# R loaded through POOL's queue, its spread moved up on DVE, and thirteen identity products on PE before the first projection

## The reference, cut to what matters

```
q, k, v = (split_heads(xn @ W.T + b) for W, b in ((Wq, bq), (Wk, bk), (Wv, bv)))     # xn = layernorm(x)
feature_map(t) = exp(t/sqrt(8) @ R - 0.5 * sum((t/sqrt(8))**2))                       # R is 8 x 8
q1, k1 = feature_map(q), feature_map(k)
kv = einsum('bhnd,bhne->bhde', k1, v);  z = 1 / (sum(q1) + 1e-8)
x = x + merge(einsum('bhnd,bhde,bhn->bhne', q1, kv, z)) @ Wo.T + bo
x = x + cross(layernorm(x), experts(slots(layernorm(x))))
```

## Time and profile before

| what | us |
|---|---|
| median of the three runs | 193.84 |
| the profiled execution | 194.13 |
| its span, first to last instruction | 192.3 |
| PE busy | 176.7 (92%) |
| POOL busy | 140.7 (73%) |
| DVE busy | 135.7 (71%) |
| ACT busy | 117.4 (61%) |

### The profile page before, as it was taken

How to read it: one execution, slowest core, us unless ns; L and a number is a source line. 1 busy time by engine, 2 the same in 40 slices (tenths; PEclk the granted TensorE clock), 3 DMA queues, 4 the chain that set the end, 5 groups by cost and what they waited for, 6 DMA issues and landing times.

```text
span 192.3 us, 4773 instructions
## 1 busy us (share of the span) xinstructions
PE 176.7 (92%) x1495; PEld 131.1 (68%) x1495; DVE 135.7 (71%) x399; ACT 117.4 (61%) x292; POOL 140.7 (73%) x278
## 2 busy tenths in 40 slices
PE   0798879999999999999999976999998999999993
PEld 0435567778876777777878755732665699888992
DVE  2668958797877887869786634637527999979850
ACT  2235357796779858776977562236413876765871
POOL 4488969879789986899276695305957869687983
PEclk9999999999999999999999997599999999999999
DMA  4839968999990000000000000000000000201113
GB/s 108 239 101 366 362 152 262 346 349 335 367 311 14 0 3 2 3 0 3 0 3 0 2 5 0 0 3 0 3 0 0 0 27 32 84 29 59 55 56 111
DMA packets 19675, 18.25 MB, mean 95 GB/s; under 512 B 1289, under 2 KB 15458, under 8 KB 19650
## 3 DMA queue, kind: packets, MB, share of 16 engines
q1 hardware_dynamic: 18802, 17.35, 28.7%
q10 hardware_dynamic: 848, 0.59, 1.4%
HBM read 15.84 MB, written 2.10 MB: 93 GB/s over the span
## 4 chain that ended last, share of the span: by engine, by line
PE 75%; POOL 11%; DVE 3%; issue 3%; DMA 3%; ACT 2%; ACTq 1%; POOLq 0%; DVEq 0%
PE ps L1131 11%; PE ps L1203 8%; PE ps L1372 6%; PE ps L1418 5%; PE ps L1241 4%; PE ps L1310 4%; PE ps L1184 4%; PE ps L1141 4%; PE ps L1164 3%; PE ps L1154 3%; PE ps L1406 3%; DMA X<-in_L_attn_x_dram 3%; PE ps L1395 2%; PE ps L1195 2%; PE ps L1174 2%
## 5 line engine op out<-in xcount | busy, mean ns | idle before, releaser
L1131 PE MATMUL ps<-Wproj,xnT 128*128 128x512 f32 x64 | 32.5, 633 | 1.0 <-ACT Wproj L544 0.5
L508 POOL TENSOR_TENSOR Wgs<-Wgs,W2s 128x256 f32<-128x256 f32 x31 | 18.7, 628 | 1.5 <-DVE W2s L1030 1.5
L1131 PEld LDWEIGHTS ps<-Wproj,xnT 128*128 128x128 f32 x64 | 11.4, 198 | 10.0 <-issue 8.6
L1418 PE MATMUL ps<-W1s,W2s 128*128 128x128 f32 x128 | 17.3, 279 | 0.7 <-ACT W2s L705 0.7
L1418 PEld LDWEIGHTS ps<-W1s,W2s 128*128 128x128 f32 x128 | 15.8, 191 | 2.2 <-ACT W2s L705 1.8
L1203 PE MATMUL ps<-XN2T,Ad 128*128 128x256 f32 x64 | 16.7, 384 | 0.1
L439 POOL TENSOR_SCALAR xn<-X,nm,rs 128x127 f32<-128x127 f32 x32 | 14.8, 471 | 1.5
L517 POOL TENSOR_TENSOR W2s<-W2s,X 128x256 f32<-128x256 f32 x15 | 10.8, 728 | 6.3 <-ACT W2s L711 3.3
L577 ACT ACTIVATE pr<-ps,nmax 128x256 f32<-128x256 f32 x32 | 14.9, 475 | 0.3 <-DVE nmax L888 0.2
L584 ACT ACTIVATE sq<-ps 128x512 f32<-128x512 f32 x16 | 9.6, 597 | 8.5 <-PE ps L1131 8.1
L849 DVE TENSOR_REDUCE ss<-sq 128x64 f32<-128x512 f32 x16 | 10.9, 682 | 5.3 <-ACT sq L584 5.0
(11 more groups left out here) (189 smaller groups left out, 487.8 us busy)
## 6 DMA issues: line engine op xcount, KB each, us to landing
W1s<-in_L_ffn_e_W_dram SPq DMA_DIRECT2D x4, 1024.0 KB, 8.1
Wgs<-in_L_ffn_e_Wg_dram SPq DMA_DIRECT2D x4, 1024.0 KB, 8.3
W2s<-in_L_ffn_e_W_dram SPq DMA_DIRECT2D x16, 256.0 KB, 8.3
out_dram<-W2s SPq DMA_DIRECT2D x16, 128.0 KB, 1.7
X<-in_L_attn_x_dram SPq DMA_DIRECT2D x3, 512.0 KB, 6.1
X<-in_L_attn_x_dram ACTq DMA_DIRECT2D x2, 128.0 KB, 2.5
X<-in_L_attn_x_dram ACTq DMA_DIRECT2D x1, 256.0 KB, 5.2
W<-in_L_ffn_e_b_dram SPq DMA_DIRECT2D x3, 32.0 KB, 1.8
```

The lines of the kernel that those rows point to most:

```text
L508: last = pool.tensor_tensor(heads(at[:, k, j * HS:(j + 1) * HS], S), heads(ep[:, k, j * HS:(j + 1) * HS], S), over(rsm[:, k, j * H:(j + 1) ...
L1131: last = pe.matmul(banks(b)[:, j, :], xnT[:, k, j * P:(j + 1) * P], Wproj[:, :], start=True, stop=True)
L1418: last = pe.matmul(ps[:, 6 + b % 2, j * P:(j + 1) * P], atT[:, b % RING, hf, j * P:(j + 1) * P], VWs[:, hf, b, :], start=(hf == 0), stop=( ...
```

## The change

The load of R is moved from ACT's queue to the front of POOL's stream, ahead of the identity matrix, so POOL's own queue issues it, and ACT issues X of batches 2 and 3 one place sooner. On DVE spread_rotation goes ahead of apply_first. On PE a new function warm(n) multiplies the identity by itself n times into columns 0 to 127 of PSUM bank 2, which nobody reads: ten times ahead of turn_biases, once behind turn_xn(0), and twice behind feature_weights. Its first call waits for ident.

```diff
@@ gpsimd
+            load(pool, r_in, (Rrep[:, :], R.unsqueeze(0).broadcast_to([H, DH, DH])))
             own(pool.memset(ident[:, :], 0.0))
@@ scalar
             sc.dma_start(X[:, 1:2, :], x_rows[:, 1:2, :]).then_inc(x_in[4], 16)
-            load(sc, r_in, (Rrep[:, :], R.unsqueeze(0).broadcast_to([H, DH, DH])))
             sc.dma_start(X[:, 2:4, :], x_rows[:, 2:4, :]).then_inc(x_in[5], 16)
@@ vector
-            stats1(0); moments1(0); center_weights(); set_biases(); apply_first(); spread_rotation(); stats1(1)
+            stats1(0); moments1(0); center_weights(); set_biases(); spread_rotation(); apply_first(); stats1(1)
@@ tensor
+            def warm(n):
+
+                pe.wait_ge(ident_ok, 1)
+                for _ in range(n):
+                    pe.matmul(ps[:, 2, 0:P], ident[:, :], ident[:, :], start=True, stop=True)
+
@@
-            turn_biases(); turn_weights(); turn_xn(0); feature_weights(); project(0); turn_xn(1)
-            turn_value_weights(); project(1); key_sums(0); turn_xn(2); key_values(0); project(2)
+            warm(10); turn_biases(); turn_weights(); turn_xn(0); warm(1); feature_weights(); warm(2); project(0)
+            turn_xn(1); turn_value_weights(); project(1); key_sums(0); turn_xn(2); key_values(0); project(2)
```

## The result

| | before | after |
|---|---|---|
| median of nine runs each | 194.1 | 195.04 |
| the profiled execution | 194.13 | 195.06 |
| its span | 192.3 | 193.3 |

The medians differ by 0.94 us (a ratio of 1.0048), and every one of the nine times after (194.73 to 195.8) lies above every one of the nine before (192.6 to 194.6). The ratio on record, which is not that of the medians, is 1.0072 [1.0051, 1.0094]: of 194.1 that is 1.4 us, between 1.0 and 1.8. So the change is slower by less than 1%, clear of the scatter, and its size is known only as about 0.9 to 1.8 us. The forecast was 194.9 within 193.0 to 196.9, and slower by 1.06.

What follows compares the result with a forecast made beforehand. POOL's chain from 11.31 to 26.40 us was taken to bound PE's start. The lead's delay through DVE gave POOL +1.04; +1.0 on the profiled 194.13 made 195.2, as a median 194.9, range 193.0 to 196.9.

Steps and rivals of the forecast that it cites:

- What bounds the kernel: The chain of waits never leaves POOL between 11.31 and 26.40 us, then releases PE; whatever moves POOL's 11.31 moves the end.
- one rival only: The clock isn't held or doesn't rise before the projection; POOL late by 2.0 us, 195.9 in all; chance 0.17.
- POOL's issue: On POOL, issuing R's load ahead of the identity takes 0.69 us (ends 0 and 1.28), so ident is ready at 2.22.
- the 1.58 from which batch 0 would have been late: Idle behind POOL's start; rival: a longer issue also delays batch 0's factors, at 2.5 us +2.8, 196.6; chance 0.12.
- The lead: On PE, warm(10) is 20 records from about 2.3, taking 4.1 us; turn_biases starts at 6.4 instead of 3.90.
- DVE behind it: DVE waits for turn_biases, then copies, spread and apply_first; stats1(1) starts at 8.1 instead of 6.32, 1.8 us later.
- POOL's chain: POOL normalises batches 2 and 3 at 8.1 + 2.84 + 1.41 = 12.35 instead of 11.31, +1.04 us.
- R and X: R lands at 4.7, ahead of its use at 7.2; X of batches 2 and 3 lands at 7.43, which buys nothing.
- "no wait for R": On DVE, the wait for R (0.45 us of idle at 6.11) is gone, since R lands at 4.7.
- The clock and the first projection: PE's clock rises after 3.9 us; the projection runs from 9.8 to 11.8, 1.8 us won there and lost in front.
- The rival of a clock that has not risen before the projection: The projection runs 10.9 to 14.7, 2.8 us later; POOL late by 2.0: 195.9, or 196.5 with issue 1.28; chance 0.17.
- the late stretch: Around 120 us the clock is at 0.50; rival: this dip goes, 2.4 us less, 192.5; chance 0.08.

Runs made afterwards that it cites:

- the first and the fifth experiment: First: the changed kernel without its thirteen products, 194.33. Fifth: the kernel before with POOL's masks and cleared rows moved to its idle stretches around the first norm factors, 194.05.

## Why the prediction was right, point by point

**What bounds the kernel.** Right. The chain of waits went from POOL's norms to PE as described, and turn_xn2(0) moved by just what POOL's normalising moved. What the prediction left out is the second chain, which the first and the fifth experiment found: its reciprocal is ready only 0.76 us before POOL asks for it in the kernel before, and in those two experiments POOL waited 0.40 and 2.02 us for it, so this chain takes most of any gain. The 0.76 stood in the earlier trace rows and was used in one rival only.

**POOL's issue.** Predicted 0.69 of delay to ident, measured 1.32 (ident ends at 2.85 for 1.53): the issue is 0.76, near the row of ACT that stood for it, but the stream also starts 0.53 later (1.32 for 0.79). The sum had no term for that. It stayed under the 1.58 from which batch 0 would have been late.

**The lead.** Predicted 4.1 us up to turn_biases, measured 4.56. All twenty records are at 0.21; the prediction let the last ones run at the higher clock, and they did not, in that execution. With R on SP it was nearly as predicted: the clock rose inside the lead, and turn_biases came 4.19 behind its start. With the products alone it was 4.57. Together with the start 0.6 later, turn_biases was 1.06 later than forecast (7.46 against 6.4).

**DVE behind it.** Predicted 1.72 us from turn_biases to stats1(1), measured 1.16. Of the 0.56 between them, 0.20 is the first copy: it starts 0.30 behind turn_biases, and not 0.50, since in the kernel before DVE was still busy with center_weights (3.84 to 4.29) and the 0.50 was not PE's alone. The other 0.36 is that the working added durations from the rows. In the trace, steps that follow one another on DVE overlap: the spread starts 0.15 after the first copy, apply_first 0.20 later, stats1(1) 0.51 after that, where the durations are 0.16, 0.28 and 0.60. So half of the earlier misses came back: stats1(1) at 8.62 against 8.1.

**POOL's chain.** Predicted 4.25 us from stats1(1) to the normalising of batches 2 and 3, measured 4.26. Delay +1.57 against +1.04.

**R and X.** R was forecast to land at 4.7. Without the lead to cover it, it lands at 5.7 (1.33 and 4.38 us): half of the miss is that it starts 0.53 later, half that it takes 4.4 us and not the 3.9 of ACT's queue. With the lead it was in by 5.9 (1.32 and 4.6), still ahead of its use at 7.91, so "no wait for R" held with less to spare than forecast. X was forecast to land at 7.43 and landed at 7.3 (2.20 and 5.1). That it buys nothing behind the lead held. What X is worth is seen with R on SP.

**The clock and the first projection.** Forecast some 2.0 us from 9.8, measured 2.26 from 11.44. The clock rose not at the end of the lead but during the projection's first record. The Trainium skill ("TensorE: Matmul & The Clock Gate", Part 1), which the prediction used, says that the array starts at the lower clock, and the trace agrees (twenty records in 4.63 us). The moment of the rise is read from the records. The rival of a clock that has not risen before the projection was half true, and of no weight: the projection ended 1.8 us later than before (13.70 for 11.92), but POOL was late by itself and reached its first scaling (19.74) 0.56 us after the reciprocal was ready (19.18).

**The end.** Of +1.58 in the profiled pair, 0.58 came back in the late stretch at 1.2 GHz. The prediction priced that stretch as all or nothing, at 2.4 us and a chance of 0.08. It comes in two lengths instead, in both kernels, and the forecast had no term for which one a run gets.

So the mechanism and the sign held: the lead ahead of turn_biases holds DVE and POOL, the issue on POOL adds to it, and both lie on the path. The size held with luck. The shift at PE was 0.54 larger than forecast, out of misses of 0.6 (POOL's start and issue) and 0.5 (the lead) one way and 0.56 (DVE) the other. By the medians (+0.94) the forecast of +1.06 looks nearly exact, by the ratio (+1.4) it is low. Why the medians show less than the 1.58 of the profile stays open; the 0.58 of the late stretch explains it for the profiled pair alone.

## What to carry to other kernels

Filler products belong only in idle time that ends no earlier than they do: the engine's stream is in order, and what stands behind the filler may release engines that the filler never touches. A faster step off the path pays nothing: the first projection took 1.9 to 2.0 us instead of 3.78 in four of these kernels, and none of their medians is below that of the kernel before. Where that projection had lain on the path (R on POOL with the spread first and no products), shortening it helped X2 in one profile, that of the lead behind the biases: 25.98 for 26.43. Work that is moved out of a gap may have hidden a late load or a second chain, so look at what the engine would wait for next before taking the gap for a gain.

## What the runs showed of the hardware

- **A small load's queue changes its neighbours.** R is 4 KB. With R on SP, X of batches 2 and 3 (256 KB, from ACT's queue) lands in 2.9 to 3.3 us. With R ahead of it on ACT it takes 4.4 to 5.4, and with R on POOL 4.7 to 5.1. The median of the two 128 KB loads of X (batches 0 and 1) is 2.5 to 2.8 us with R on ACT or SP, and 3.5 to 3.8 with R on POOL. R itself takes 3.3 to 3.5 us on SP, 3.9 to 4.3 on ACT, 4.4 to 4.8 on POOL. Each range is over all profiles with that queue.
- **POOL's stream starts later when it opens with a load:** 1.32 to 1.33 instead of 0.79 to 0.80. Why stays open.
- **The first rise of the clock varies.** The same twenty records ahead of turn_biases end at the lower clock in two profiles (4.63 and 4.64 us) and with a rise inside them in a third (4.26); directly behind turn_biases, in a fourth, they take 3.98 with a rise inside. The granted clock reads 1.00 at 8 to 9 us before and after alike, where the projection's records are still at the slow spacing or have not begun; before the first rise only the records' spacing shows the level.
- **The clock falls again after idle time.** In the two kernels in which PE stood idle for 3.07 and 2.94 us near 18 to 21 us, the granted clock is 0.50 from 22 to 24 us. Before, where PE waited 0.34 us at that step, it is 1.00.
- **The late stretch at 1.2 GHz comes in two lengths.** It is 6.8 us in the profile before and 3.4 in the one after, and the mean granted clocks of the other executions (0.982 or 0.991) say by estimate that each kernel has both. The executions of the kernel before whose mean granted clock is 0.991 are about 0.9 us shorter than those with 0.982. A comparison of two single executions of this kernel is therefore good to no better than that.
